# Attention's four value products of a head group in one run

## The reference

```python
# 8 batches x 4 key/value heads, 4 query heads on each, 512 tokens, 16 channels a head
scores = jnp.einsum('bgrqd,bgkd->bgrqk', qg, k) * SCALE
scores = jnp.where(causal, jnp.finfo(scores.dtype).min, scores)
attn = jax.nn.softmax(scores, axis=-1)
out = jnp.einsum('bgrqk,bgkd->bgrqd', attn, v)
```

## Time and profile before

| | us |
|---|---|
| median of 3 runs | 2398.47 |
| lowest and highest run | 2396.58, 2403.39 |
| the profiled execution | 2402.66 |
| its span, first to last instruction | 2401.0 |
| first attention (layer 2): first and last exponential start at | 402.3, 687.4 |
| second attention (layer 3): the same | 1470.5, 1762.0 |
| PE busy over the span | 2084.7 (87%) |
| DVE busy | 1642.8 (68%) |
| ACT busy | 1280.1 (53%) |
| POOL busy | 711.1 (30%) |

### The profile page before, as it was taken

The page is one execution under the profiler, slowest core; times in us unless marked ns, Lnnn a source line. Parts: engine busy times, 40 slices in busy tenths (PEclk is TensorE's granted clock), DMA queues, the critical chain, the costliest instruction groups (busy, mean ns, idle before and its releaser), DMA issues. The chain is left out here.

```text
span 2401.0 us, 44539 instructions
## 1 busy us (share of the span) xinstructions
PE 2084.7 (87%) x15328; PEld 1612.0 (67%) x15328; DVE 1642.8 (68%) x3066; ACT 1280.1 (53%) x2221; POOL 711.1 (30%) x688
## 2 busy tenths in 40 slices
PE   5969777999986899869998567999985499999998
PEld 4758633555555788769998223454454399999998
DVE  2867756787835776636665697777735777777775
ACT  2434443666653444235554233666642088888885
POOL 1423200232310000037886001222310145555553
PEclk8989888999998899979999787999987799999999
DMA  3000024221203000086565343122104367777774
GB/s 124 1 0 0 0 80 111 55 57 51 58 1 111 1 1 1 22 200 103 116 98 66 103 109 79 52 58 50 50 1 129 123 202 223 221 223 221 220 223 96
DMA packets 176772, 218.55 MB, mean 91 GB/s; under 512 B 34057, under 2 KB 152498, under 8 KB 176242
## 3 DMA queue, kind: packets, MB, share of 16 engines
q1 hardware_dynamic: 146290, 175.19, 23.8%
q0 software_dynamic: 30336, 41.44, 10.6%
HBM read 161.25 MB, written 54.79 MB: 90 GB/s over the span
## 5 line engine op out<-in xcount | busy, mean ns | idle before, releaser
L1414 ACT ACTIVATE L_attn_probs<-L_attn_ps_t 128x512 f32<-128x512 f32 x640 | 370.2, 599 | 233.6 <-PE L_attn_ps_t L1332 228.5
L1314 PE MATMUL L_attn_ps_m<-L_attn_k,L_attn_q 96*128 96x512 bf16 (+3 forms) x1024 | 277.5, 312 | 35.0 <-DMA L_attn_k<-L_k_parts 29.3
L1279 POOL TENSOR_SCALAR_AFFINE_SELECT L_attn_probs<-L_attn_probs 128x512 f32<-128x512 f32 x256 | 153.3, 635 | 452.9 <-ACT L_attn_probs L1414 452.9
L1332 PE MATMUL L_attn_ps_t<-L_attn_q,L_attn_k 98*128 98x512 bf16 (+3 forms) x1024 | 245.7, 301 | 3.4 <-ACT L_attn_probs L1414 3.1
L1314 PEld LDWEIGHTS L_attn_ps_m<-L_attn_k,L_attn_q 96*128 96x128 bf16 x1024 | 102.2, 100 | 205.1 <-issue 156.2
L2462 POOL DMA_INDIRECT out<-L_experts_result,L_moe_give x78 | 161.3, 2068 | 208.5 <-DVE L_experts_result L2634 196.6
L1455 DVE TENSOR_REDUCE L_attn_top<-L_attn_ps_m 128x2 f32<-128x1024 f32 x128 | 156.6, 1223 | 73.7 <-PE L_attn_ps_m L1316 71.5
L1316 PE MATMUL L_attn_ps_m<-L_attn_causal,L_attn_ident 128*128 128x128 bf16 x1024 | 198.4, 225 | 0.0
L1356 PE MATMUL L_attn_ps_v<-L_attn_probs,L_attn_v 128*32 128x512 f32 (+3 forms) x2048 | 193.5, 453 | 3.6 <-POOL L_attn_probs L1279 3.0
L2741 POOL DMA_INDIRECT L_experts_token<-L_moe_rows,L_moe_take x80 | 81.6, 1019 | 377.4 <-POOLq L1778 325.2
L2480 PE MATMUL L_experts_ps_y<-L_experts_w_high,L_experts_hT_low 128*128 128x256 f32 x624 | 179.6, 288 | 0.0
(11 more groups left out here) (435 smaller groups left out, 6042.8 us busy)
## 6 DMA issues: line engine op xcount, KB each, us to landing
L_staged_w<-L_ffn_w SPq DMA_DIRECT2D x78, 1024.0 KB, 7.7
L_attn_q<-L_q_parts SPq DMA_DIRECT2D x64, 192.0 KB
L_attn_q<-L_q_parts SPq DMA_DIRECT2D x64, 128.0 KB
L_moe_rows<-L_moe_ln_normed SPq DMA_DIRECT2D x16, 512.0 KB, 3.0
L_q_parts<-L_qkv_q_parts SPq DMA_DIRECT2D x32, 192.0 KB, 2.9
L_q_parts<-L_qkv_parts SPq DMA_DIRECT2D x32, 192.0 KB, 3.1
load_ring<-x SPq DMA_DIRECT2D x8, 512.0 KB, 4.0
L_attn_q<-L_q_parts SPq DMA_DIRECT2D x64, 64.0 KB
```

The costliest lines, as they stand in the source:

```text
L1279: return pool.affine_select(out=block, in_=block, compare_op=ALU.is_ge, fill=0.0, base=0, pattern=columns, channel_multiplier=-1)
L1314: pe.matmul(bank[:, at:at + width], q[j][0:96, head, qb * P:(qb + 1) * P], k[j][0:96, 0:width], start=True, stop=False)
L1332: last = pe.matmul(bank[:, at:at + width], k[j][0:98, kb * P:(kb + 1) * P], q[j][0:98, head, kb * P:S], start=True, stop=True)
L1414: act.activation(probs[j % 2][:, place[unit], :], ps_t[:, n % 2, :], ACT.Exp, scale=scale).then_inc(exped, 1)
```

## The change

All four value products are issued after piece 8 of the next unit. The order among them, their operands and all other instructions stay.

```diff
-    TOPS_AT, TURN_AT, WEIGH_AT = 2, 5, (4, 6, 8, 9)
+    TOPS_AT, TURN_AT, WEIGH_AT = 2, 5, {7: (0, 1, 2, 3)}
...
                         if n in WEIGH_AT and weigh:
-                            weigh_values(u - 1, (j + 3) % 4, WEIGH_AT.index(n), first_weigh)
+                            for kb in WEIGH_AT[n]:
+                                weigh_values(u - 1, (j + 3) % 4, kb, first_weigh)
```

## The result

The changed kernel takes 2422.94 us (median of four runs, 2421.42 to 2424.75) beside 2398.61 us before: 24.3 us more, a ratio of 1.0099 with a 95% interval of 1.0081 to 1.0116. The profiled execution has a span of 2423.0 us.

A forecast was written before the change was run, and what follows sets the result against it. TensorE was taken as the bound, without slack, VectorE close behind. A loop of 9.47 us, from 9.08 and 9.26, over 28 units a layer adds 10.9 and 5.9, +17 us on 2398.47: 2415 us, range 2403 to 2430.

The forecast's parts named there:

- the walk: One round of the unit's loop from block's end to block's end, steps read from rows: 9.47 us, bounds 9.31 and 9.72.
- the wait at the turn: After piece 6, TensorE's output turn waits about 0.7 us for VectorE's split, no longer covered by the 512-column run.
- the late exponential and reduce at piece 3: TensorE reaches piece 3's scores at 2.44 us, waits for an exponential to 2.94; maxima wait some 0.3 for sweep 5's reduce.
- handing back: From the end of VectorE's split to the start of TensorE's output turn: 0.06 us.
- The bound of 0.1 us for transpositions that start after a wait: Upper allowance of 0.1 us for the output turn's four transpositions starting after a wait, not in a stream.
- The saved switches: Three of four value runs' fixed costs disappear, 0.25 us each: 0.75 us a unit.
- The inner changes of key block: Three steps between key blocks inside the block of value products: taken as zero, upper bound 0.05 us each.
- Layer 3 and layer 2 at one pace: Layer 3's extra VectorE operation falls in the block, so both layers take 9.47 us, from 9.26 and 9.08.
- Rival 1: Saved switches are paid out, TensorE stays the bound: 8.33 us a unit, 2351 us; chance 0.07 including its milder case.
- Its middle case: Only the output turn's wait absent, piece 3's wait stays: 8.79 us a unit, 2377 us; within the shared chance 0.07.
- Rival 2: No difference that shows: hand-offs overlap, loop 9.31 us or less, up to 7 us more, 2405 us or less; chance 0.12.
- Rival 3: The block is no single run, each inner change keeps its drain: 10.22 us a unit, 2457 us; chance 0.05.

The follow-up runs named there:

- the version with one run: Changed kernel with all four value products in one block after piece 10 and VectorE's split of the maxima ahead of sweep 2's reduce: 2364.26 us.
- the version with two runs: Changed kernel with the 512-column value products back after piece 5, the other three together after piece 10, the output turn after piece 7: 2359.72 us.
- the kernel with the split ahead: Changed kernel with VectorE's split of the row maxima ahead of the reduce of sweep 2, TensorE's order untouched: 2384.35 us.
- the first run late: Kernel before the change, with only the 512-column value products moved from after piece 5 to after piece 7: 2430.28 us.
- the block after piece 10: Changed kernel with the one block of value products after piece 10 in place of piece 8: 2390.95 us.

## Why the prediction was right

The direction, the mechanism and the range held; the predicted 2415 us were 8 us short. Both losses of the change stand in the walk: the wait at the turn, and the late exponential and reduce at piece 3. It can be read step by step in the timeline of the changed kernel, from the end of one block to the end of the next:

```profile
513.97 0.34 PE L1314 MATMUL L_attn_ps_m<-L_attn_k,L_attn_q 96*128 96x384 bf16 x1
...
514.88 0.38 PE L1332 MATMUL L_attn_ps_t<-L_attn_q,L_attn_k 98*128 98x256 bf16 x2
...
516.27 2.91 ACT L1415 ACTIVATE L_attn_probs<-L_attn_ps_t 128x512 f32<-128x512 f32 x5
...
516.93 0.39 PE L1332 MATMUL L_attn_ps_t<-L_attn_q,L_attn_k 98*128 98x512 bf16 x1
...
517.55 0.22 PE L1316 MATMUL L_attn_ps_m<-L_attn_causal,L_attn_ident 128*128 128x128 bf16 x1
...
517.80 0.96 DVE L1458 TENSOR_REDUCE L_attn_top<-L_attn_ps_m 128x2 f32<-128x768 f32 x1 [0.30 <-PE L_attn_ps_m L1316]
...
519.31 0.28 DVE L1472 TENSOR_TENSOR L_attn_top_rows<-L_attn_ps_o,L_attn_top_rows 16x128 bf16<-16x128 f32 x1
...
519.74 0.63 PE L1369 MATMUL L_attn_ps_o<-ident,L_attn_oT 128*128 128x128 f32 x4 [0.63 <-DVE L_attn_top_rows L1472]
520.20 0.38 PE L1314 MATMUL L_attn_ps_m<-L_attn_k,L_attn_q 96*128 96x512 bf16 x1
...
520.70 0.38 PE L1314 MATMUL L_attn_ps_m<-L_attn_k,L_attn_q 96*128 96x512 bf16 x1
...
521.29 2.36 PE L1356 MATMUL L_attn_ps_v<-L_attn_probs,L_attn_v 128*32 128x512 f32 x32
...
523.58 0.34 PE L1314 MATMUL L_attn_ps_m<-L_attn_k,L_attn_q 96*128 96x384 bf16 x1
```

| step | predicted | measured |
|---|---|---|
| block's end to the scores of piece 10 | 0.89 | 0.91 |
| to the next unit's first exponential | 1.39 | 1.39 |
| to the scores of piece 3 | 0.66 | 0.66 |
| to the last maximum product of sweep 2, and its reduce | 0.87 | 0.87 |
| reduce and split | 1.79 | 1.79 |
| handing back to the output turn | 0.06 | 0.15 |
| output turn | 0.44 | 0.46 |
| pieces 7 and 8, and the gap ahead of the block | 1.10 | 1.09 |
| the block | 2.27 | 2.29 |
| sum | 9.47 | 9.61 |

**The term that was too small** is the handing back. I took 0.06 us from a score matmul that waits for ScalarE; the transposition started 0.15 us after the split's end. The bound of 0.1 us for transpositions that start after a wait covered it. That is 0.09 of the 0.14 us by which the walk was short; the rest is 0.02 us in each of three steps, less 0.01 in a fourth. 0.14 us in 28 units of two layers is the 8 us. Mostly for the same reason the turn lost 0.80 us where about 0.7 were forecast.

**The saved switches.** Four runs with their gaps were 2.72 + 0.40 = 3.12 us, the block with its gap is 2.29 + 0.09 = 2.38 us: 0.74 us saved, where 0.75 were forecast. The inner changes of key block cost nothing, as the rows at half clock had said. At a granted clock of 1.00, the 2.4 GHz level, the loads of weights stand 0.43, 0.32 and 0.32 us apart, two cycles a column for 512, 384 and 384 columns:

```profile
512.13 0.13 PEld L1356 LDWEIGHTS L_attn_ps_v<-L_attn_probs,L_attn_v 128*32 128x32 f32 x4 [0.30 <-issue]
512.56 0.13 PEld L1356 LDWEIGHTS L_attn_ps_v<-L_attn_probs,L_attn_v 128*32 128x32 f32 x4 [0.30 <-issue]
...
512.88 0.13 PEld L1356 LDWEIGHTS L_attn_ps_v<-L_attn_probs,L_attn_v 128*32 128x32 f32 x4 [0.19 <-issue]
513.20 0.56 PEld L1356 LDWEIGHTS L_attn_ps_v<-L_attn_probs,L_attn_v 128*32 128x32 f32 x12 [0.19 <-issue]
```

The trace agrees with the Trainium skill's TensorEngine Tiling (Array Packing), Key Properties, that a change of tiling mode drains TensorE and a change of tile alone doesn't, as far as times show it: 0.25 us a run at the changes of mode, nothing inside the block. The Trainium skill's warning on the same page, under PSUM Bottleneck, that tiling speeds TensorE up but not the emptying of PSUM, fits only in part: in the version with one run TensorE loses 0.26 us a unit to VectorE's reduces, but those empty the maxima, whose products aren't tiled (96*128 in the rows).

**Layer 3 and layer 2 at one pace** came as forecast, 9.61 each. The wait at piece 3 for the second reduce of sweep 5 is 9.7 us in 27 units, 0.36 us; 0.3 was forecast. These rows, like the earlier trace rows, give idle time of the loading of weights: before, layer 3 showed the same 0.36 us a unit and was only 9.26 - 9.08 = 0.18 us slower. ScalarE's gap at piece 9 (2.4 us) and VectorE's at sweep 5 (1.6 us) are as forecast. The DMAs of the split maxima, put 1.5 us later in the unit, left 2.54 us after the transposition of the maxima in both kernels (501.52 to 504.06, and 517.15 to 519.69).

**The rivals.** Rival 1's price was real: the version with two runs is paid it for both runs it saves, and in the change the waits spend it. Its middle case, the turn's wait gone and the wait at piece 3 left, was put at 8.79 us and 2377 us; the kernel with the split ahead is that case, at 8.79 us and 2384 us. The other 7 us don't show in the pace, and where they lie stays open. Rival 2 would have needed hand-offs that overlap, and they didn't. Rival 3 fell with the block's 2.29 us.

## What to carry to other kernels

Before work on the pacing engine is gathered in one place, ask what each piece of it was covering: a run between a producer and its consumer is slack for another engine's chain, and 1.1 us of such cover, 0.80 us a unit when it went, was worth as much here as three saved mode switches. A closed loop over three queues, each step read from one row of the trace, gave the new pace within 0.14 us of 9.61, though the engines' busy shares say nothing of it. When a gathering loses, look for the hand-off that it uncovered, and for engines that start late behind the block: moving the turn by one piece, or the split by one place in VectorE's queue, took the loss away. Keeping the covering run, gathering the rest at the end of the unit and turning one piece later took 38 us off the kernel. And read the price of a wait from start to start: the idle time listed was 0.63 us where 0.80 were lost, and 0.36 in layer 3 before, where 0.18 were.

## What the runs showed of the hardware

An fp32 transposition that waits for VectorE started 0.15 us after the last operation's end, in all 56 units of both layers in which the turn waits, in each of three kernels (the change, the first run late, the block after piece 10). A 16-bit score matmul that waits for ScalarE starts after 0.06 us. The engine waited for doesn't make the difference. In the changed kernel the 16-bit maxima of piece 3 start 0.06 us after VectorE's reduce ends (515.95 + 0.41 = 516.36, then 516.42), and the transposition's load of weights begins only 0.12 us after the split's end (519.59 to 519.71). So most of the difference arises ahead of that load; why, no run isolates.
